# Graph attention on one core: who fetches the source rows of a group's chunks

## The chip, the core and the metric
The kernel runs on one core of a Trainium2 chip. The core has TensorE (PE), VectorE (DVE), ScalarE (ACT), GpSimd (POOL) and SyncE (SP), each with its own queue of instructions; all start DMAs onto the same 16 DMA engines. What counts is the device time of one execution in microseconds (us), as the median of several runs.

## What is computed
A graph with 6250 nodes of 128 features and 200,000 edges, sorted by destination, goes through two layers: a SAGE layer (mean over neighbours, two matrix products, a norm), then a graph attention layer with 4 heads of 32 channels. The attention layer is what matters here:

```python
x_l = (x @ W).reshape(N, H, C)
logits = leaky_relu(a_src[src_all] + a_dst[dst_all] + a_edge, 0.2)
m = segment_max(logits, dst_all)
p = exp(logits - m[dst_all])
alpha = p / segment_sum(p, dst_all)[dst_all]
out = segment_sum(alpha[:, :, None] * x_l[src_all], dst_all)
```

So for each edge the row `x_l[src]` of its source node is needed, 132 numbers (four heads of 32 channels and the head's `a_src`), 528 bytes, at a place in memory that only the data tell.

## The kernel before
The work is a row of stages; the one that the diff touches is `attention` (from line 2089), and after it comes `finish`. Edges are laid out in chunks of 128 with one edge per partition, and 15 chunks (`J`) make a group; there are 108 groups (`N_GRP`). Every engine runs the same loop over groups, unrolled 12 times (`UN`), so nine rounds; `u` is a group's place in its round. The engines meet through semaphores alone.

For a group `g`:
- **GpSimd** (line 2270) waits for `s_i` (the indices of the group are copied) and `s_ms` (its buffer is free), then issues one indirect DMA per chunk (line 2277) that gathers 128 rows of `x_tab` into a slot of `G`. `G` has room for four groups of 15 slots and two slots more. In the groups with u = 5 and 11 it leaves out the first chunk.
- **SyncE** (line 2217) issues, in each step, the load of the one-hot rows `OHT` three groups ahead (line 2222, 480 KB, in a ring of three), after a wait for `s_x`, which tells that matmuls have read the slot's last tenant. It also fetches the chunks that GpSimd leaves out: line 2255 loads that chunk's list of 128 source numbers from `src_pad` into `numbers`, line 2241 loads 16 of these at a time into registers, and line 2246 issues one DMA for each row, 16 in a part. A list is loaded at the beginning of six steps, ahead of that step's one-hots; the eight parts are spread over the six steps as 2, 2, 1, 2, 1, 0. `starts` holds where each list begins, loaded before the loop in 18 DMAs of one number (line 2229).
- **ScalarE** (line 2283) builds the one-hots of the next group from `OHT` (lines 2295, 2297), copies the indices for the group three ahead (line 2328, this signals `s_i`) and the keys `KB` (2286), then in `turned` waits for TensorE and copies `ADG` and `KT` (2302, 2306), copies edge terms (2336), and takes the exponentials `f1` (2338) and of `DL` into `PR` (2340) and `MSG` (2341). It issues no DMA in this stage.
- **TensorE** turns the logits `L` (2392), gathers destination terms (2348, and in `spread` 2363 into `px`) and sums messages by one-hot matmuls into `pu` (2375). `spread` signals `s_x`.
- **VectorE** multiplies rows with weights (`messages`, 2439, signals `s_ms`), adds up `LP` (2530, 2533), waits for the gathers of the group (`s_g`, and in groups u = 5 and 11 also `s_sr` for SyncE's rows), forms the logits `L` (2541, 2544), scans them for segment maxima (2548, 2551), builds one-hots (2433) and adds the sums of `pu` to `ACC` (2468), 15 times a group.

Before the loop, ScalarE and VectorE wait for `AE` (line 2230, 3.4 MB).

Of the kernel before, what the change touches and what calls it, by code (L numbers as in the profile page):

```python
# [149 lines left out]
def build(nc, x, src, dst, edge_attr, W1l, W1r, b1, W2l, W2r, b2, gamma, beta,  # L150
          W, W_edge, att_src, att_dst, att_edge, bias, out):
    with ExitStack() as top:
# [31 lines left out]
        rel_tab = nc.dram_tensor("rel_tab", [NK, P], BF16).ap()  # L184
        blk_tab = nc.dram_tensor("blk_tab", [1, NK], I16).ap()
        a_tab = nc.dram_tensor("a_tab", [NSL, P, N_BLK * P], BF16).ap()
        x_keep = nc.dram_tensor("x_keep", [P, NB, D], F32).ap()
# [1901 lines left out]
        def attention(at, block):  # L2089
# [7 lines left out]

            BY_SP = 6
            assert UN % BY_SP == 0 and BY_SP % 4 == 2
            s_sr = [sem(f"a_sr{u}", at) for u in range(UN // BY_SP)]  # L2100
            s_st = sem("a_st", at)
            s_nu = sem("a_nu", at)
            s_g = s_src
            s_i = sem("a_i", at)
# [44 lines left out]
            idx = sb("idx", [P, 4, J], I32, at)  # L2149
            G = sb("G", [P, 4 * J + 2, XW], F32, at)  # L2150
            starts = sb("starts", [1, N_GRP // BY_SP], I32, at)
            numbers = sb("numbers", [1, P], I32, at)
            OH = sb("OH", [P, 4, J, P], F32, at)
            OHT = sb("OHT", [P, 3, J, P], BF16, at)
# [37 lines left out]

            def by_sync(u):
                return u % BY_SP == BY_SP - 1

            def places(u):

                at_ = (0, J + 1, 2 * J + 1, 3 * J + 2)[u % 4] - (1 if by_sync(u) else 0)
                return G[:, at_:at_ + J, :]

            def fetched(i, u, last=J):

                n = [J - 1 if by_sync(v) else J for v in range(u % 4, UN, 4)]
                return 16 * (sum(n) * i + sum(n[:u // 4]) + last - (1 if by_sync(u) else 0))

# [9 lines left out]


            @block.sync
            def _(sp):
                lists = rel_tab[0:N_GRP * J].rearrange("(g j) e -> g (j e)", j=J)

                def rows_of(g, k):
                    sp.dma_start(OHT[:, k].rearrange("p j f -> p (j f)"),
                                 lists[bass.ds(g, 1), :].to_broadcast([P, J * P])).then_inc(s_rb[k], 16)

                for g in range(3):
                    rows_of(g, g)
                for r in range(N_GRP // BY_SP):
                    k = (BY_SP * r + BY_SP - 1) * J
                    sp.dma_start(starts[:, r:r + 1], ek4i[k % P:k % P + 1, k // P:k // P + 1]).then_inc(s_st, 16)
                sp.dma_start(AE[:], ae_t).then_inc(s_ael, 16)  # L2230
                sp.wait_ge(s_bz, 1)
                with nc.allow_non_contiguous_dma(reason="groups of 15 numbers"):
                    sp.dma_start(BLK[:, 2:N_GRP + 2, 0:J], blk_tab[:, 0:N_GRP * J].rearrange("o (g j) -> o g j", j=J)
                                 ).then_inc(s_bl, 16)
                sp.wait_ge(s_st, 16 * (N_GRP // BY_SP))
                flat_s = src_pad.rearrange("(o e) -> o e", o=1)
                SPAN = BY_SP - 1
                PART = 16

                def node_rows(u, at_):  # L2240
                    _, v = nc.values_load_multi_w_load_instructions(
                        numbers[0:1, at_:at_ + PART], engines=(mybir.EngineType.SP,), min_val=0, max_val=NV - 1,
                        skip_runtime_bounds_check_because="the sources are numbers of nodes")
                    for n in range(PART):
                        p = at_ + n
                        sp.dma_start(places(u)[p:p + 1, 0, :], x_tab[bass.ds(v[n], 1), :]
                                     ).then_inc(s_sr[u // BY_SP], 16)

                def round_of(i, last):
                    for half in range(UN // BY_SP):  # L2250
                        r = i * (UN // BY_SP) + half
                        u = BY_SP * half + BY_SP - 1
                        hold(sp, s_ms, BY_SP * r + 1)
                        e = sp.value_load(starts[0:1, bass.ds(r, 1)], min_val=0, max_val=(E_PAD - P) * HEADS)
                        sp.dma_start(numbers[:], flat_s[:, bass.ds(e // HEADS, P)]).then_inc(s_nu, 16)
                        for n in range(BY_SP):
                            if not last or BY_SP * half + n + 3 < UN:
                                sp.wait_ge(s_x, BY_SP * r + n + 4)
                                rows_of(BY_SP * r + n + 3, n % 3)
                            if n == 0:  # L2260
                                hold(sp, s_nu, 16 * (r + 1))
                            for at_ in range(0, P, PART):
                                if at_ // PART * SPAN // (P // PART) == n:
                                    node_rows(u, at_)

                with sp.Fori(0, N_GRP // UN - 1) as i:
                    round_of(i, False)
                round_of(N_GRP // UN - 1, True)

            @block.gpsimd  # L2270
            def _(pool):

                def step(i, u, g, left):
                    pool.wait_ge(s_i, g + 1)
                    hold(pool, s_ms, g + 1)
                    for j in range(1 if by_sync(u) else 0, END if left == 0 else J):
# [7 lines left out]
            def _(act):  # L2284
# [32 lines left out]
                turned(0)  # L2317
                act.wait_ge(s_ael, 16)

                def step(i, u, g, left):  # L2320
# [110 lines left out]
            def _(dve):  # L2431
# [5 lines left out]
                def messages(g, u, n=J):  # L2437
                    dve.wait_ge(s_p, g + 2)
                    dve.tensor_tensor(MSG[:, u % 2, 0:n, 0:XW].rearrange(x_l, h=HEADS)[:, :, :, 0:C_HEAD],  # L2439
                                      places(u % UN)[:, 0:n].rearrange(x_l, h=HEADS)[:, :, :, 0:C_HEAD],  # L2440
                                      jh(PR)[:, 0:n, :, None].to_broadcast([P, n, HEADS, C_HEAD]),
# [78 lines left out]
                def step(i, u, g, left):  # L2520
# [232 lines left out]
```

## Time and profile before

| | |
|---|---|
| median of three runs | 3497.34 us (3493.5, 3497.34, 3505.45) |
| the profiled execution, its own time | 3505.29 us |
| its span | 3503.3 us |
| VectorE busy | 2590.7 us |
| GpSimd busy | 1924.0 us |
| ScalarE busy | 1596.4 us |

The profile shows one execution. Its page gives each engine's busy time (register work, waits and issuing of DMAs do not count), the span in 40 slices, and the costliest groups of instructions by line. The list of waits says which engine waited before which line and what ended the wait. The timeline has one row per instruction or run of equal ones: start, duration, engine, line, operation, tiles, and in brackets the idle time ahead of it with its releaser. SPq and ACTq are issues of DMAs by SyncE and ScalarE, with the time of the issue, not of the transfer. A gather of GpSimd counts as DMA_INDIRECT on POOL.

### The profile page before, as it was taken

The page shows a single profiled execution, that of the slowest core. Times are in us where ns is not written, and L with a number is a line of the kernel's source. Part 1 is how long each engine was busy: PE and PEld are TensorE (multiplying, and loading weights), DVE is VectorE, ACT ScalarE, POOL GpSimd, SP SyncE. Part 2 cuts the span into 40 slices and gives each one's busy share as a digit, 9 for nine tenths or more (in the row PEclk, how much of TensorE's full clock was granted, in tenths as well). Part 3 has the DMA queues.
Part 4 walks back from the last instruction along what each step waited for, and adds up shares of the span by engine and source line. Part 5 has one row for each costly group of instructions (what it writes and reads, how often), then busy time and mean ns, then how long its engine had stood idle before and what let it go on. Part 6 is the DMA issues. An engine that isn't in the chain of part 4 may idle for free. (4 is left out here: it accounts for less than half of the span.)

```text
span 3503.3 us, 69699 instructions
## 1 busy us (share of the span) xinstructions
PE 2347.6 (67%) x19840; PEld 1970.9 (56%) x19840; DVE 2590.7 (74%) x6998; ACT 1596.4 (46%) x2523; POOL 1924.0 (55%) x1954
## 2 busy tenths in 40 slices
PE   5799999999998899455445545545555455455453
PEld 5687777888777777454444444444444444444443
DVE  4799999994576764687777767767777777777677
ACT  4587778885455556333333333333333333332331
POOL 5441111341114322477777777777777777777773
PEclk9999999999999999666665666656565665666655
DMA  5243333672378888433333333333333333333335
GB/s 171 92 168 152 140 141 151 184 172 94 120 267 250 258 256 249 155 90 79 85 84 81 82 84 84 81 82 84 84 79 84 84 79 84 85 84 78 84 78 97
DMA packets 172054, 432.24 MB, mean 123 GB/s; under 512 B 44750, under 2 KB 95768, under 8 KB 163308
## 3 DMA queue, kind: packets, MB, share of 16 engines
q1 hardware_dynamic: 62352, 271.13, 21.0%
q0 software_dynamic: 66064, 128.62, 18.9%
q10 hardware_dynamic: 43244, 27.80, 2.8%
q8 instruction: 179, 2.93, 0.4%
q14 instruction: 215, 1.76, 0.2%
HBM read 308.87 MB, written 120.11 MB: 122 GB/s over the span
## 5 line engine op out<-in xcount | busy, mean ns | idle before, releaser
L2277 POOL DMA_INDIRECT G<-x_tab,idx x1593 | 1508.5, 947 | 485.6 <-issue 485.3
L2375 PE MATMUL pu<-MSG,OH 128*128 128x140 f32 x3282 | 733.3, 395 | 26.9 <-DVEq L2505 16.4
L2375 PEld LDWEIGHTS pu<-MSG,OH 128*128 128x128 f32 x3282 | 670.7, 289 | 36.4 <-DVE ACC L2468 17.1
L2468 DVE TENSOR_TENSOR ACC<-pu,ACC 128x140 f32 x1641 | 484.1, 295 | 127.7 <-PE pu L2375 75.9
L2392 PE MATMUL pc<-ident,L 128*60 128x128 f32 x108 | 42.2, 391 | 799.1 <-DVE L L2544 789.1
L2392 PEld LDWEIGHTS pc<-ident,L 128*60 128x60 f32 x108 | 13.6, 126 | 827.1 <-issue 827.1
L961 ACT CAST AE<-psA 128x784 bf16<-128x784 f32 x496 | 397.5, 815 | 127.0 <-PE psA L994 126.0
L2302 ACT CAST ADG<-pt 128x180 bf16<-128x180 f32 x108 | 103.2, 955 | 708.4 <-PE pt L2348 702.2
L1095 DVE TENSOR_TENSOR OHL<-iol,LH 128x2048 bf16<-128x2048 bf16 (+1 forms) x248 | 358.1, 1444 | 24.2 <-PE psA L994 17.3
L1644 ACT CAST AR<-AE 128x896 fp32r<-128x896 bf16 x248 | 243.2, 1017 | 197.7 <-PE psR L1838 119.3
L1005 PE MATMUL psR<-SPL,AE 128*128 128x384 bf16 x1736 | 322.9, 326 | 0.0
L1838 PE MATMUL psR<-SPR,AR 128*128 128x256 f32 x1922 | 282.8, 295 | 10.5 <-ACT AR L1644 10.4
L994 PE MATMUL psA<-OHH_c,OHL 128*128 128x98 bf16 (+1 forms) x4800 | 259.6, 201 | 23.3 <-DVE OHH_c L1095 23.0
L1838 PEld LDWEIGHTS psR<-SPR,AR 128*128 128x128 f32 x1922 | 248.9, 193 | 23.5 <-ACT AR L1644 15.2
L2541 DVE TENSOR_TENSOR L<-G,LP 128x60 f32<-128x60 f32 x108 | 27.7, 257 | 313.3 <-DMA G<-x_tab,idx 313.3
L994 PEld LDWEIGHTS psA<-OHH_c,OHL 128*128 128x128 bf16 x4800 | 218.9, 98 | 72.0 <-DVE OHH_c L1095 35.9
L2439 DVE TENSOR_TENSOR MSG<-G,pq 128x1920 f32<-128x1920 f32 (+1 forms) x109 | 231.6, 2125 | 25.8 <-issue 25.8
L1095 DVE TENSOR_TENSOR OHH_c<-ioh,LH 128x1568 bf16<-128x1568 bf16 (+1 forms) x248 | 241.4, 973 | 0.0
L907 POOL DMA_INDIRECT srows<-src_pad,EKI x38 | 65.8, 1732 | 318.2 <-DVE KB L1077 188.5
L2433 DVE TENSOR_TENSOR OH<-pq,REL 128x1920 f32<-128x1920 f32 x108 | 232.0, 2148 | 0.0
L1830 PE MATMUL psR<-SPB,AE 128*128 128x384 bf16 x1116 | 217.6, 332 | 12.3 <-DMA AE<-a_tab 10.5
L2338 ACT ACTIVATE f<-f 1x4 f32<-1x4 f32 x108 | 22.1, 204 | 433.1 <-DVE f L2581 425.0
(432 smaller groups left out, 4453.2 us busy)
## 6 DMA issues: line engine op xcount, KB each, us to landing
a_tab<-AE SPq DMA_DIRECT2D x62, 1568.0 KB
OHT<-rel_tab SPq DMA_DIRECT2D x108, 480.0 KB, 3.9
AE<-a_tab SPq DMA_DIRECT2D x60, 800.0 KB, 6.2
AE<-a_tab SPq DMA_DIRECT2D x60, 768.0 KB, 8.6
G<-x_tab SPq DMA_DIRECT2D x2304, 0.5 KB
G<-x_tab,idx POOLq DMA_INDIRECT x1593
at_in<-in_edge_attr SPq DMA_DIRECT2D x26, 250.0 KB
SUMS<-in_edge_attr ACTq DMA_DIRECT2D x24, 250.0 KB
```

Source lines behind the costliest of these rows:

```text
L961: act.copy(A[i % 2][:, :, UN_S * u:UN_S * (u + 1)].rearrange("p h (k s) -> p k h s", k=2), psA[:, n % 2, :, 0:W8].rearrange("p k (s h) -> ...
L994: mm = pe.matmul(psA[:, n % 2, c * w // W8, to:to + w], OHL[:, m % RING, k], OHH[:, m % RING, k * step:k * step + w], start=True, stop=True)
L1005: pe.matmul(psR[:, i % 2, 0:3 * D], A[i % 2][:, h, :], SPL[:, h].rearrange("p s f -> p (s f)"), start=(h == 0), stop=False)
L1095: return dve.tensor_tensor(out.rearrange("p (s h t) -> p s h t", s=k, t=2), columns[:, 0:w].rearrange("p (h t) -> p h t", t=2)[:, None].to ...
L1644: act.copy(AR[:, n % 3, 0:len(rows_)], A[i % 2][:, rows_[0]:rows_[-1] + 1]).then_inc(s_cs, 1)
L1830: mm = pe.matmul(psR[:, i % 2, 0:3 * D], A[i % 2][:, h, :], SPB[:, h].rearrange("p s f -> p (s f)"), start=(h == 0), stop=False)
L1838: mm = pe.matmul(psR[:, i % 2, 0:2 * D], AR[:, n % 3, k], SPR[:, h - N_BF].rearrange("p s f -> p (s f)"), start=False, stop=(h == N_BLK - 1))
L2277: pool.indirect_dma_start(places(u)[:, j, :], None, x_tab, bass.IndirectOffsetOnAxis(ap=idx[:, u % 4, j:j + 1], axis=0)).then_inc(s_g[u % ...
L2375: mm = pe.matmul(pu[:, k[0], k[1]:k[1] + MW], OH[:, u % 4, j, :], MSG[:, u % 2, j, :], start=True, stop=True)
L2433: dve.tensor_tensor(OH[:, u % 4], rowq[:, None, :].to_broadcast([P, J, P]), REL[:, bass.ds(g * J, J)][:, :, None].to_broadcast([P, J, P]), ...
L2439: dve.tensor_tensor(MSG[:, u % 2, 0:n, 0:XW].rearrange(x_l, h=HEADS)[:, :, :, 0:C_HEAD], places(u % UN)[:, 0:n].rearrange(x_l, h=HEADS)[:, ...
L2468: dve.tensor_tensor(a, pu[:, k[0], k[1]:k[1] + MW][:, None, :], a, ALU.add).then_inc(s_c, 1)
```

## The change
SyncE now fetches a chunk in every fourth group (u = 3, 7, 11) instead of every sixth. A list is used in four steps with two parts in each, and it is loaded in the first of them, behind the one-hots, with the wait for it right behind its issue. The rows for u = 3 of a round are issued in the last two steps of the round before and the first two of its own, and so on, two steps ahead of their use; for the first list, two parts stand before the loop. ScalarE fetches a chunk of the group u = 9: it loads the list in step 0 of a round and issues 16 rows in each of the steps 1 to 8, between `keys` and `turned`. GpSimd gathers the others: 176 instead of 178 chunks in a round. The start of every chunk's list is now brought to one partition by a write of all 1664 numbers to a table in memory and a load of it, in place of the 18 DMAs. `G` has one slot more, and its layout changes so that the chunks fetched apart have slots that earlier groups don't use.

```diff
-            BY_SP = 6
+            BY_SP = 4
...
+            BY_ACT, PART_A = 9, 16
...
+            def chunk_apart(u):
+                if u % UN == BY_ACT:
+                    return 0
+                return None if u % 4 != 3 else 0 if u % UN == UN - 1 else J - 1
...
+            def list_of(eng, to, k, signal):
+                e = eng.value_load(starts[0:1, bass.ds(k, 1)], min_val=0, max_val=(E_PAD - P) * HEADS)
+                eng.dma_start(to[:], flat_s[:, bass.ds(e // HEADS, P)]).then_inc(signal, 16)
+
+            def node_rows(eng, kind, to, u, at_, n, signal):
+                _, v = nc.values_load_multi_w_load_instructions(
+                    to[0:1, at_:at_ + n], engines=(kind,), min_val=0, max_val=NV - 1,
+                    skip_runtime_bounds_check_because="the sources are numbers of nodes")
+                for m in range(n):
+                    eng.dma_start(places(u)[at_ + m:at_ + m + 1, chunk_apart(u), :], x_tab[bass.ds(v[m], 1), :]
+                                  ).then_inc(signal, 16)
...
+                    sp.dma_start(ek_tab.rearrange("c p -> p c"), ek4i[:]).then_inc(s_ek, 16)
                 for g in range(3):
                     rows_of(g, g)
-                for r in range(N_GRP // BY_SP):
-                    k = (BY_SP * r + BY_SP - 1) * J
-                    sp.dma_start(starts[:, r:r + 1], ek4i[k % P:k % P + 1, k // P:k // P + 1]).then_inc(s_st, 16)
+                sp.wait_ge(s_ek, 16)
+                sp.dma_start(starts[:], ek_tab.rearrange("c p -> (c p)").rearrange("(o f) -> o f", o=1)
+                             ).then_inc(s_st, 16)
                 sp.dma_start(AE[:], ae_t).then_inc(s_ael, 16)
...
+                def part(r, u, n):
+                    if n == 0:
+                        list_of(sp, numbers, (BY_SP * r + 3) * J + chunk_apart(u), s_nu)
+                        hold(sp, s_nu, 16 * (r + 1))
+                    for m in range(2):
+                        node_rows(sp, mybir.EngineType.SP, numbers, u, 32 * n + 16 * m, 16, s_sr[u // BY_SP])
 
                 def round_of(i, last):
+                    for n in range(UN):
+                        g = UN * i + n
+                        if not last or n + 3 < UN:
+                            sp.wait_ge(s_x, g + 4)
+                            rows_of(g + 3, n % 3)
+                        q = n + 2
+                        if not last or q < UN:
+                            if q % BY_SP == 0:
+                                hold(sp, s_ms, g + 2)
+                            part(UN // BY_SP * i + q // BY_SP, (q // BY_SP * BY_SP + 3) % UN, q % BY_SP)
+
+                for n in range(2):
+                    part(0, 3, n)
...
-                    for j in range(1 if by_sync(u) else 0, END if left == 0 else J):
+                    for j in gathered(u, END if left == 0 else J):
...
+                def rows_apart(i, u, g):
+                    if u == 0:
+                        list_of(act, numbers_a, g * J + BY_ACT * J, s_na)
+                    elif (u - 1) * PART_A < P:
+                        if u == 1:
+                            act.wait_ge(s_ms, g + 2)
+                            hold(act, s_na, 16 * (i + 1))
+                        node_rows(act, mybir.EngineType.Activation, numbers_a, BY_ACT, (u - 1) * PART_A, PART_A, s_ar)
...
                         keys(g + 1)
+                        rows_apart(i, u, g)
                         turned(g + 1)
...
-                    if by_sync(u):
+                    if u % BY_SP == 3:
                         dve.wait_ge(s_sr[u // BY_SP], 16 * P * (i + 1))
+                    if u == BY_ACT:
+                        dve.wait_ge(s_ar, 16 * P * (i + 1))
```

## Rows read from the trace of the kernel before

**Rows 1.** the page, busy us, share of the span and instructions of each engine
```profile
PE 2347.6 (67%) x19840; PEld 1970.9 (56%) x19840; DVE 2590.7 (74%) x6998; ACT 1596.4 (46%) x2523; POOL 1924.0 (55%) x1954
```

**Rows 2.** list of waits, 1540 to 3440 us: engine, line, releaser; us, times, longest
```profile
POOL G L2277 <- issue: 462.5, 1517, 0.3
...
DVE L L2541 <- DMA G<-x_tab,idx: 313.3, 95, 4.5
```

**Rows 3.** view of line 2277: duration ns min/median/max, first and last start us
```profile
L2277 POOL DMA_INDIRECT G<-x_tab,idx x1593: 940/944/1113, 1445.7 to 3438.6; - x200
```

**Rows 4.** timeline of VectorE, line 2541: start us, us; groups 10, 22 and 107
```profile
1670.20 0.26 DVE L2541 TENSOR_TENSOR L<-G,LP 128x60 f32<-128x60 f32 x1 [2.95 <-DMA G<-x_tab,idx]
...
1893.08 0.26 DVE L2541 TENSOR_TENSOR L<-G,LP 128x60 f32<-128x60 f32 x1 [2.96 <-DMA G<-x_tab,idx]
...
3449.11 0.26 DVE L2541 TENSOR_TENSOR L<-G,LP 128x60 f32<-128x60 f32 x1
```

**Rows 5.** timeline of SyncE, one step of its loop that waits for nobody
```profile
2593.06 0.36 SPq L2222 DMA_DIRECT2D OHT<-rel_tab  x1
2594.80 14.33 SPq L2246 DMA_DIRECT2D G<-x_tab  x32
2609.38 0.36 SPq L2222 DMA_DIRECT2D OHT<-rel_tab  x1
```

**Rows 6.** timeline of ScalarE, the two pauses in group 2498 to 2517
```profile
2509.50 0.95 ACT L2302 CAST ADG<-pt 128x180 bf16<-128x180 f32 x1 [6.61 <-PE pt L2348]
...
2514.83 0.20 ACT L2338 ACTIVATE f<-f 1x4 f32<-1x4 f32 x1 [4.08 <-DVE f L2581]
```

**Rows 7.** timeline of SyncE at the start of the stage
```profile
1445.57 10.65 SPq L2229 DMA_DIRECT2D starts<-ek4i  x18
...
1470.63 14.77 SPq L2246 DMA_DIRECT2D G<-x_tab  x32
```

**Rows 8.** timeline of SyncE around two issues of the list, within and across rounds
```profile
1553.65 0.36 SPq L2222 DMA_DIRECT2D OHT<-rel_tab  x1
1555.22 0.27 SPq L2255 DMA_DIRECT2D numbers<-src_pad  x1
...
1662.89 0.36 SPq L2222 DMA_DIRECT2D OHT<-rel_tab  x1
1668.26 0.27 SPq L2255 DMA_DIRECT2D numbers<-src_pad  x1
```

**Rows 9.** the page, DMA issues: KB each, median us from issue to landing
```profile
OHT<-rel_tab SPq DMA_DIRECT2D x108, 480.0 KB, 3.9
```

**Rows 10.** timeline of SyncE, the last 64 rows
```profile
3390.90 30.62 SPq L2246 DMA_DIRECT2D G<-x_tab  x64
```

**Rows 11.** timeline of VectorE, line 2541, groups 0 and 5
```profile
1483.07 0.26 DVE L2541 TENSOR_TENSOR L<-G,LP 128x60 f32<-128x60 f32 x1
...
1558.66 0.26 DVE L2541 TENSOR_TENSOR L<-G,LP 128x60 f32<-128x60 f32 x1 [0.93 <-DMA G<-x_tab,idx]
```

**Rows 12.** list of DMA issues of ScalarE, two kinds that are small
```profile
x_tab<-H ACTq DMA_DIRECT2D x1, 66.0 KB, 1.6
...
b1c<-in_L_gnn_b ACTq DMA_DIRECT2D x1, 1.0 KB, 12.2
```

**Rows 13.** views of lines 2241 and 2246: SyncE loading 16 numbers, issuing a row
```profile
L2241 SPq TENSOR_LOAD <-numbers x144: 1137/1180/1407, 1469.3 to 3413.4; - x144
...
L2246 SPq DMA_DIRECT2D G<-x_tab x2304: 224/228/293, 1470.6 to 3421.3; - x192
```

**Rows 14.** view of line 2452: VectorE loading eight block numbers
```profile
L2452 DVEq TENSOR_LOAD <-BLK x219: 1823/1828/2056, 1470.4 to 3451.9; - x110
```

**Rows 15.** views of lines 2722, 2654 and 2658: both engines issuing after the stage
```profile
L2722 SPq DMA_DIRECT2D X<-x_keep x3: 363/425/427, 3468.1 to 3468.9; - x3
...
L2654 ACTq DMA_DIRECT2D H<-x_tab x4: 407/528/532, 3467.8 to 3469.3; - x4
...
L2658 ACTq DMA_DIRECT2D H<-x_tab x9: 374/851/1611, 3470.6 to 3477.6; - x9
```

More of the change, by code:

```diff
@@ L185, in build @@
         blk_tab = nc.dram_tensor("blk_tab", [1, NK], I16).ap()
+        ek_tab = nc.dram_tensor("ek_tab", [KC, P], I32).ap()
         a_tab = nc.dram_tensor("a_tab", [NSL, P, N_BLK * P], BF16).ap()
@@ L2095, in attention @@
             assert N_GRP % UN == 0
-            BY_SP = 6
-            assert UN % BY_SP == 0 and BY_SP % 4 == 2
+            BY_SP = 4
             s_sr = [sem(f"a_sr{u}", at) for u in range(UN // BY_SP)]
+            s_ek = sem("a_ek", at)
             s_st = sem("a_st", at)
             s_nu = sem("a_nu", at)
+            BY_ACT, PART_A = 9, 16
+            s_ar = sem("a_ar", at)
+            s_na = sem("a_na", at)
             s_g = s_src
@@ L2149, in attention @@
             idx = sb("idx", [P, 4, J], I32, at)
-            G = sb("G", [P, 4 * J + 2, XW], F32, at)
-            starts = sb("starts", [1, N_GRP // BY_SP], I32, at)
+            G = sb("G", [P, 4 * J + 3, XW], F32, at)
+            starts = sb("starts", [1, NK], I32, at)
             numbers = sb("numbers", [1, P], I32, at)
+            numbers_a = sb("numbers_a", [1, P], I32, at)
             OH = sb("OH", [P, 4, J, P], F32, at)
@@ L2191, in jh, with gathered @@
                 return t.rearrange("p h j -> p j h")
-            def by_sync(u):
-                return u % BY_SP == BY_SP - 1
+            def chunk_apart(u):
+                if u % UN == BY_ACT:
+                    return 0
+                return None if u % 4 != 3 else 0 if u % UN == UN - 1 else J - 1
             def places(u):
-                at_ = (0, J + 1, 2 * J + 1, 3 * J + 2)[u % 4] - (1 if by_sync(u) else 0)
+                if u % 4 == 3:
+                    at_ = 3 * J + {UN - 1: 1, 3: 2, 7: 3}[u % UN]
+                else:
+                    at_ = (0, J + 1, 2 * J + 1)[u % 4] - (1 if u % UN == BY_ACT else 0)
                 return G[:, at_:at_ + J, :]
+            def gathered(u, last=J):
+                return [j for j in range(last) if j != chunk_apart(u)]
             def fetched(i, u, last=J):
-                n = [J - 1 if by_sync(v) else J for v in range(u % 4, UN, 4)]
-                return 16 * (sum(n) * i + sum(n[:u // 4]) + last - (1 if by_sync(u) else 0))
+                n = [len(gathered(v)) for v in range(u % 4, UN, 4)]
+                return 16 * (sum(n) * i + sum(n[:u // 4]) + len(gathered(u, last)))
             def steps(eng, body):
@@ L2213, in steps @@
                     body(rounds, u, UN * rounds + u, UN - 1 - u)
+            flat_s = src_pad.rearrange("(o e) -> o e", o=1)
+            def list_of(eng, to, k, signal):
[8 more added lines that the diff above has]
+                                  ).then_inc(signal, 16)
             @block.sync
@@ L2223, in rows_of @@
                                  lists[bass.ds(g, 1), :].to_broadcast([P, J * P])).then_inc(s_rb[k], 16)
+                with nc.allow_non_contiguous_dma(reason="chunks lie along partitions"):
+                    sp.dma_start(ek_tab.rearrange("c p -> p c"), ek4i[:]).then_inc(s_ek, 16)
                 for g in range(3):
                     rows_of(g, g)
-                for r in range(N_GRP // BY_SP):
-                    k = (BY_SP * r + BY_SP - 1) * J
-                    sp.dma_start(starts[:, r:r + 1], ek4i[k % P:k % P + 1, k // P:k // P + 1]).then_inc(s_st, 16)
+                sp.wait_ge(s_ek, 16)
+                sp.dma_start(starts[:], ek_tab.rearrange("c p -> (c p)").rearrange("(o f) -> o f", o=1)
+                             ).then_inc(s_st, 16)
                 sp.dma_start(AE[:], ae_t).then_inc(s_ael, 16)
@@ L2234, in _ @@
                                  ).then_inc(s_bl, 16)
[L2235 to L2247, printed above, removed]
@@ L2249, in round_of @@
-                def round_of(i, last):
[L2250 to L2264, printed above, removed]
+                hold(sp, s_st, 16)
@@ L2318, in _ @@
                 act.wait_ge(s_ael, 16)
+                act.wait_ge(s_st, 16)
+                def rows_apart(i, u, g):
[6 more added lines that the diff above has]
+                        node_rows(act, mybir.EngineType.Activation, numbers_a, BY_ACT, (u - 1) * PART_A, PART_A, s_ar)
                 def step(i, u, g, left):
@@ L2439, in messages @@
                     dve.tensor_tensor(MSG[:, u % 2, 0:n, 0:XW].rearrange(x_l, h=HEADS)[:, :, :, 0:C_HEAD],
-                                      places(u % UN)[:, 0:n].rearrange(x_l, h=HEADS)[:, :, :, 0:C_HEAD],
+                                      places(u)[:, 0:n].rearrange(x_l, h=HEADS)[:, :, :, 0:C_HEAD],
                                       jh(PR)[:, 0:n, :, None].to_broadcast([P, n, HEADS, C_HEAD]),
```

## The prediction

> **What bounds the kernel now.** The page's busy shares come first [rows 1]: no engine is busy for more than 74% of the span, so averages don't name the bound. The stage that the diff touches is `attention`, 108 groups of up to 15 chunks in about 2000 us of the 3503. The list of waits in the stage does [rows 2]: VectorE waits for a landing of `G` before line 2541 in 95 groups, 313.3 us in all, so some 3.3 us a group, while GpSimd's only waits are "issue", 0.3 us before each gather. The view of line 2277 says the same from the other side [rows 3]: 1593 gathers from 1445.7 to 3438.6 us, so one in 1.252 us (944 ns and the gap). GpSimd issues without a pause and is the clock of the stage. Line 2541 confirms it [rows 4]: between 1670.20 and 1893.08 us, twelve groups or one round of the loop, lie 222.88 us, and the 178 gathers of a round at 1.252 us make 222.9.
>
> Two other clocks run close behind, and the change loads both. SyncE issues the rows that GpSimd doesn't gather. Where it waits for nobody, a step with 32 rows takes 2609.38 - 2593.06 = 16.3 us [rows 5], against 222.88 / 12 = 18.6 us for a group. ScalarE has two pauses in a group, 6.6 us before `ADG` and 4.1 us before `f` [rows 6].
>
> **What is taken from GpSimd.** Before, two groups in twelve (u = 5, 11) lack a gather: 178 in a round. After, u = 3, 7, 11 and 9 lack one: 176. In nine rounds that is 18 gathers fewer, 1575 in all, and 18 x 1.252 = 22.5 us. The rest of GpSimd's step is unchanged: its waits on `s_i` and `s_ms` were met ahead. All 22.5 us lie on the path as long as the next clock is slower by no more than that, so the stage's last full wait, and with it the last `L`, moves from 3449.1 us [rows 4] to 3426.6.
>
> **SyncE, the main question.** A step of its loop issues the rows of one-hots (line 2222), then up to 32 rows. Before, a list served six steps, with 2, 2, 1, 2, 1 and 0 parts of 16 rows. The full steps were followed by lighter ones. Now a list serves four steps, each with two parts. Four steps cost:
> - Four full steps. 16.3 each where all runs freely [rows 5]; but the 32 rows themselves take 14.33 to 14.77 us [rows 5, 7], so I take 16.6 and have 66.5, with 65.3 as the lower bound.
> - The list. Without a turn of the loop, `numbers` is issued 1.57 us after the rows of one-hots, of which 0.36 is their own issue: 1.2 us [rows 8]. Before, it was issued ahead of the next one-hots and a whole step's wait hid its landing. Now it is issued behind them, on the same queue, and `hold` on `s_nu` follows at once. One-hots take 3.9 us from issue to landing [rows 9]; a list behind them lands no earlier, so at least 3.9 - 1.6 = 2.3 us are waited. If it takes a whole such landing of its own it is 3.9. With the 1.2 that is 3.5 to 5.1; I take 4.0, nearer the first, as the list is one row of 0.5 KB against 480.
> - The turn of the loop. 1668.26 - 1662.89 = 5.37 us where it is otherwise 1.57 [rows 8]: 3.8 us in twelve steps, 1.3 in four.
> Together 71.8 us, bounds 70.1 and 72.9.
>
> GpSimd's four groups will cost (222.88 - 2.5) / 3 = 73.5 us. So SyncE fits, by 2%. It also starts late: its first list waits behind the load of `AE`, and rows start at 1470.63 [rows 7]. Now 64 rows come before the loop, where one-hots of group 3 were issued at once; 64 rows take 30.6 us [rows 10]. So the loop's first step begins near 1501.3. One-hots of group 3 go out there, 16 us or so ahead of ScalarE's use; the rows of groups 3 and 7 come some 5 to 10 us after GpSimd's, which VectorE makes good, since its own work is (1558.66 - 0.93 - 1483.07) / 5 = 14.9 us a group while it waits for nobody [rows 11]. Rows of the last group are out after 106 steps, 26.5 fours: 1501.3 + 26.5 x 71.8 + 1.6 for landing (the fastest landing of a plain DMA [rows 12]) = 3405.6, against 3426.6. The break-even is (3426.6 - 1.6 - 1501.3) / 26.5 = 72.6 us in four steps. Below it SyncE costs nothing; every us above costs 26.5 us at the end.
>
> **ScalarE.** In eight of twelve steps it issues 16 rows between `keys` and `turned`. By SyncE's rows that is 1.2 us of load [rows 13] and 16 x 0.41 (14.33 us for 32 with a load between) = 7.8 us. The pause there is 6.6 us and the next, before `f`, 4.1 [rows 6]; `ADG` itself is read only by matmuls after that. So 7.8 against 10.7 us: `ADG` is late by 1 us and nobody sees it. The bounds: its load of 16 numbers may cost twice VectorE's load of 8 at 1.83 us [rows 14], which makes 10.2, still inside; nothing is gained on this side. `list_of` in step 0 is some 1.5 us in the same pause. What is queued behind it is `turned`, then the copy of `AE`, `f`, and the weights for VectorE's messages.
>
> **The start.** SyncE's 18 issues of 4 bytes, 10.65 us [rows 7], go. In their place stand a write of 1664 single numbers to `ek_tab`, a wait for it, and one load of all starts, ahead of `AE`. No row shows such a write; its bounds are 1.6 us, that fastest landing, and 12.2, a load of 256 single numbers [rows 12], so `AE` starts between some 8 us earlier and 3 later. VectorE does group 0 at 1483.07, 17 us after its gathers could be in, and waits for one again only in group 5 [rows 11]; nor is SyncE's margin of 21 us used up. So this is worth nothing; GpSimd starts as before. One more slot of `G` and a longer `starts` cost no time.
>
> **Sum.** The profiled execution has 3505.3 us for a span of 3503.3; with 22.5 less it would be 3482.8. That execution lies 8.0 above the median of the three runs, which scatter over 12. Against the median: 3497.3 - 22.5 = 3475.
>
> **Rivals.**
> A. *SyncE and ScalarE get in each other's way, and SyncE becomes the bound.* The end of the trace has both issuing at once [rows 15]: SyncE's three issues go from 363 to 427 ns, ScalarE's four from 407 to 532, while ScalarE alone has one of the same shape in 374. If an issue of SyncE's costs 62 ns more whenever ScalarE issues, that is 7.8 of 18.4 us in two steps of three, or 28% of 128 rows, 36 x 0.062 = 2.2 us in four steps; with ScalarE itself slowed to 10 us, 2.9. Then 71.8 + 2.2 = 74.0, the end moves by 26.5 x 1.4 = 37 us, and the time is 3475 + 37 = 3512: slower than before. It decides from 72.6 for a loss of gain, and from 73.45 for a loss against the kernel before. Against it: those issues are of 128 rows each, these of one row with 228 ns [rows 13], in which whatever is shared can be only a small part; with a third of that surcharge SyncE stays within 0.1 us of break-even. The same end is reached if the list lands later than 5 us after its issue.
> The Trainium skill, Perfetto Trace Analysis, section "DMA Instruction — HWDGE (DVE, Sync)", speaks for this rival: the generator of descriptors is shared and is locked for one issuer at a time, and the wait for the lock is within the time the profile gives for the issue. The longer issues at the end of the trace agree with it. If all 228 ns of a row were spent under that lock, two engines would get one row each per 456 ns, 0.045 more than SyncE's 0.41, and by the same sum the time would be 3475 + 26.5 x (71.8 + 1.6 - 72.6) = 3496.
> B. *SyncE is the bound without ScalarE's doing*, by late lists and stalls: at the upper bound of 72.9 it costs 8 us, 3483, still faster.
> C. *ScalarE is the bound.* If its rows begin only after `KB`, its load costs 3.7 us and each row 0.15 more, it issues for 12.6 us. That is 1.9 beyond the 10.7 of pauses, in 72 groups: 137 us, 3612. It decides from 10.7 us. Nothing in the trace shows ScalarE's issues slower than SyncE's by more than 20% when alone.
> D. *Nothing is gained*: gathers become dearer, or landings later, with more rows in flight. Against it: 940, 944 and 1113 ns are least, middle and most of 1593 gathers [rows 3], though SyncE's rows were in flight beside most of them. 3497.
>
> **Chances.** GpSimd stays the bound: 0.52, and 3475. SyncE the bound by little (B, and A in a mild form), up to 3487: 0.10. A between 3487 and 3508, and D: 0.16. A above 3508: 0.17. C: 0.05. For 3475 alone the range would be 3466 to 3484 by the scatter of runs; for 8 in 10 it must take in most of A, so 3466 to 3522. A measurement tells about 0.3% (10.5 us) from no change: faster 0.62, same 0.16, slower 0.22.
>
> **What would show it.** 1575 gathers at 944 ns, and line 2541 at 220.4 us per round, still waiting for GpSimd's `G`, by some 2 us more in groups of 15 than in those of 14. SyncE's step of 16.6 us, a list step of about 20.6, and SyncE still waiting now and then for `px`, though far less than before. Were A right, SyncE would hardly wait, line 2541 would wait in groups u = 3, 7, 11 for SyncE's rows, GpSimd would pause before the first gather of groups, and issues at the new line of rows would be well over 228 ns. Were C right, the pause before `f` would be gone and VectorE would wait for `px` or `PR`.

## The result and the profile after

The changed kernel takes 3483.1 us (median of six runs, 3477.7 to 3486.2); the kernel before, measured beside it, 3504.2. The ratio is 0.9938 with a 95% interval of 0.9919 to 0.9958: 21 us or 0.6% faster. The forecast was 22.5 us less, 3475 us, with a range of 3466 to 3522. The median is 8 us above the forecast because the kernel before also measured 7 us more over six runs than over the three that were known; the gain itself is 1.4 us short of the forecast.

The profiled execution has a span of 3475.5 us, 27.8 less than before. Of that, 4.8 us are not the change's: its first gather lies at 1440.85 us instead of 1445.69, though no stage ahead was edited, and in the runs below it lies anywhere from 1435.3 to 1449.9 (but for one whose edit moves it). What belongs to the change is the way from the first gather to the last `L`: 3449.1 - 1445.7 = 2003.4 us before, 3421.1 - 1440.9 = 1980.2 after, so 23.2 us less. That stretch, called "the stage" below, is the measure in all runs, since a single execution gives it to about 2 us: four executions of programs that come to the same have 1980.2 to 1982.1 (see the extra loads below). The 1980.2 of the changed kernel is the lowest of them, so its gain in the stage is 21.3 to 23.2 us.

The views of GpSimd's gathers (line 2305, was 2277 [rows 3]) and of VectorE's line for `L` (2583, was 2541), with duration in ns and first and last start:

```profile
L2305 POOL DMA_INDIRECT G<-x_tab,idx x1575: 940/944/1106, 1440.9 to 3410.6; - x197
...
L2583 DVE TENSOR_TENSOR L<-G,LP x108: 246/258/296, 1480.1 to 3421.1; 128x60 f32<-128x60 f32 x108
```

1575 gathers where there were 1593, and one in (3410.6 - 1440.9) / 1574 = 1.251 us as before. The list of waits, 1540 to 3420 us, whose counterpart is [rows 2]:

```profile
ACT ADG L2330 <- PE pt L2388: 546.4, 84, 12.6
POOL G L2305 <- issue: 455.7, 1494, 0.3
ACT f L2378 <- DVE f L2623: 367.8, 101, 4.4
DVE L L2583 <- DMA G<-x_tab,idx: 246.1, 80, 5.2
...
ACT ADG L2330 <- issue: 116.0, 19, 7.4
```

GpSimd still pauses for nothing but its own issuing. VectorE waits for its gathers 246 us instead of 313. ScalarE's two pauses had been, in the same list of the kernel before, 1540 to 3440 us:

```profile
ACT ADG L2302 <- PE pt L2348: 680.4, 102, 8.2
...
ACT f L2338 <- DVE f L2581: 400.5, 100, 4.4
```

After, 546.4 + 116.0 us are ahead of `ADG` and 367.8 ahead of `f`, but the list counts the issuing of the 1152 rows as pause. What tells of room is the releaser: in 84 groups `ADG` waits for TensorE as before, in 19 for ScalarE's own issuing. A new row of VectorE's list, over the whole stage, stands for SyncE's lateness in the first rounds:

```profile
DVE L L2583 <- DMA G<-x_tab: 45.7, 6, 9.3
```

Six groups wait for SyncE's rows (3, 7, 11, 15, 19 and 23), the last of them at 1883.67 us; none later does. Together VectorE waits 246.1 + 45.7 = 291.8 us for `G`, 21.5 less than before. What SyncE waits for, 1440 to 3420 us:

```profile
SPq L95 <- DMA numbers<-src_pad: 51.8, 27, 9.9
...
SPq L2255 <- PE px L2403: 33.4, 21, 2.4
```

All 33.4 us for TensorE's `px` lie behind 2000 us: until then SyncE, once its rows have begun, pauses for nothing but its lists. SyncE itself, in the timeline while it is behind (issue of the one-hots, of the list, of 32 rows):

```profile
1585.55 0.36 SPq L2255 DMA_DIRECT2D OHT<-rel_tab  x1
1587.28 14.62 SPq L2247 DMA_DIRECT2D G<-x_tab  x32
1602.15 0.36 SPq L2255 DMA_DIRECT2D OHT<-rel_tab  x1
1603.68 0.27 SPq L2239 DMA_DIRECT2D numbers<-src_pad  x1
1606.90 14.79 SPq L2247 DMA_DIRECT2D G<-x_tab  x32
1621.94 0.36 SPq L2255 DMA_DIRECT2D OHT<-rel_tab  x1
...
1745.85 0.27 SPq L2239 DMA_DIRECT2D numbers<-src_pad  x1
```

A full step is 16.6 us (1585.55 to 1602.15), the step with the list 19.8 (1602.15 to 1621.94). The list before this one is issued at 1534.78; three fours later comes that at 1745.85, so four steps cost 211.1 / 3 = 70.4 us, turns of the loop included. (A step with a turn takes 19.6 us instead of 16.6, so a turn costs 3.0.)

### The profile page after: what moved, and what is told of

It is laid out like the page before. It is cut to its first block and busy times, and to the rows that moved or that the text cites. A ratio compares the mean times of both kernels' runs of the same rounds, so it can differ in the third digit from the quotient of the medians.

```text
span 3475.5 us, 76894 instructions
## 1 busy us (share of the span) xinstructions
PE 2347.6 (68%) x19840; PEld 1970.5 (57%) x19840; DVE 2587.4 (74%) x6998; ACT 1596.8 (46%) x2524; POOL 1907.6 (55%) x1936
## 5 line engine op out<-in xcount | busy, mean ns | idle before, releaser
L2305 POOL DMA_INDIRECT G<-x_tab,idx x1575 | 1490.6, 946 | 480.2 <-issue 479.6
L2415 PE MATMUL pu<-MSG,OH 128*128 128x140 f32 x3282 | 734.8, 396 | 17.7 <-DVE ACC L2508 11.6
L2583 DVE TENSOR_TENSOR L<-G,LP 128x60 f32<-128x60 f32 x108 | 27.8, 257 | 291.8 <-DMA G<-x_tab,idx 246.1
L2323 ACT ACTIVATE OHT<-OHT,mine 128x1920 bf16<-128x1920 bf16 x108 | 204.1, 1890 | 12.0 <-DMA OHT<-rel_tab 12.0
```

Source lines behind the costliest of these rows:

```text
L2305: pool.indirect_dma_start(places(u)[:, j, :], None, x_tab, bass.IndirectOffsetOnAxis(ap=idx[:, u % 4, j:j + 1], axis=0)).then_inc(s_g[u % ...
L2415: mm = pe.matmul(pu[:, k[0], k[1]:k[1] + MW], OH[:, u % 4, j, :], MSG[:, u % 2, j, :], start=True, stop=True)
```

## The experiments

In each, only what is named differs from the changed kernel.

### One part alone, the other undone

Without ScalarE's part:

```diff
-                if u % UN == BY_ACT:
-                    return 0
...
-                        rows_apart(i, u, g)
...
-                    if u == BY_ACT:
-                        dve.wait_ge(s_ar, 16 * P * (i + 1))
```

> The changed kernel without ScalarE's part: GpSimd gathers the chunk of u = 9 again, 177 in a round, 1584 in all. Theory (GpSimd is the clock, every gather costs 1.252 us): from the first gather to the last L (VectorE's line after the wait for G) 1980.2 + 9 x 1.252 = 1991.5 us, a time 11 us above the changed kernel. Rival (the engines' issues get in each other's way): SyncE's step with 32 rows becomes clearly shorter than the 14.6 us of rows it has in the changed kernel, towards 14.3 or less, and its lists come closer together than 70.4 us while it is behind; the loss of ScalarE's chunk would then be partly made good, under 8 us. By the theory SyncE's pitch between rows stays at 0.411 us.

Measured: a ratio to the kernel before of 0.9985 (0.9967 to 1.0003), and a stage of 3441.2 - 1445.9 = 1995.3 us, 4 above the theory: 15 us more than the changed kernel where 11.3 were expected. Its gathers:

```profile
L2303 POOL DMA_INDIRECT G<-x_tab,idx x1584: 941/947/1123, 1445.9 to 3430.8; - x198
```

They are 947 ns long at the median instead of 944 and come one in 1.2539 us instead of 1.2514; on 1584 gathers that is 4.0 us, the whole difference. SyncE's lists, while it is behind, are issued at 1539.39 and 1608.39 us, 69.0 apart, where the changed kernel has 1603.68 - 1534.78 = 68.9; over the first three whole rounds it is 211.4, 211.3 and 211.5 us against 211.1, 211.5 and 211.1. The trace of the changed kernel shows the same row by row: of SyncE's 3456 issues 858 overlap in time with an issue of ScalarE's, and these take 229.0 ns on average, the other 2598 take 229.4. So 16 rows a step by ScalarE do not slow SyncE measurably. Rival A falls.

Without SyncE's rows:

```diff
-                return None if u % 4 != 3 else 0 if u % UN == UN - 1 else J - 1
+                return None
...
-                            part(UN // BY_SP * i + q // BY_SP, (q // BY_SP * BY_SP + 3) % UN, q % BY_SP)
...
-                    if u % BY_SP == 3:
-                        dve.wait_ge(s_sr[u // BY_SP], 16 * P * (i + 1))
```

> The changed kernel in which SyncE fetches no rows; ScalarE's chunk stays. GpSimd gathers 179 in a round, 1602 in all. Theory (GpSimd is the clock): 27 x 1.252 = 33.8 us more than the changed kernel, so 2014.0 us from the first gather to the last L, and some 11 us more than the kernel before. Rival (SyncE's rows in flight make gathers or landings dearer): the gathers come faster than one in 1.252 us and the stage is clearly shorter than 2014, say under 2008. VectorE's waits for SyncE's rows in the first rounds go.

Measured: ratio 1.0015 (0.9998 to 1.0032); the stage is 3450.6 - 1435.3 = 2015.3 us against 2014.0. Again its gathers are 947 ns long:

```profile
L2301 POOL DMA_INDIRECT G<-x_tab,idx x1602: 940/947/1089, 1435.3 to 3441.4; - x178
```

With 3456 rows fewer in flight the gathers are no cheaper, so rival D falls too: within 3 ns, the price of a gather does not hang on who else has rows under way. From this kernel to the one without ScalarE's part are 18 gathers and 20.0 us (18 pitches are 22.6, but its pitch is 1.2530 us against 1.2539, and its last `L` follows the last gather after 9.2 us instead of 10.4), from there to the changed kernel 9 gathers and 15.1, of which 4.0 are the 3 ns.

### The list issued ahead of the one-hots

```diff
+                def list_for(r, u):
+                    list_of(sp, numbers, (BY_SP * r + 3) * J + chunk_apart(u), s_nu)
...
+                        if (not last or q < UN) and q % BY_SP == 0:
+                            hold(sp, s_ms, g + 2)
+                            list_for(UN // BY_SP * i + q // BY_SP, (q // BY_SP * BY_SP + 3) % UN)
                         if not last or n + 3 < UN:
                             sp.wait_ge(s_x, g + 4)
                             rows_of(g + 3, n % 3)
```

> As the changed kernel, but SyncE issues its list ahead of the one-hots of that step, so that it lands while SyncE waits for TensorE or issues the one-hots. Theory (SyncE isn't the bound): SyncE's list step gets shorter by 2 to 3 us, so four steps cost 68 us where they cost 70.4 while it is behind, it catches up rounds earlier, and the stage is unchanged, 1980 us within 1.5. Rival (SyncE's lateness in the first rounds costs something at the end): the stage gets shorter by 5 us or more.

The stage is 3420.9 - 1439.7 = 1981.2 us: unchanged. Issues of one-hots around a list:

```profile
1533.24 0.36 SPq L2255 DMA_DIRECT2D OHT<-rel_tab  x1
1535.25 14.68 SPq L2247 DMA_DIRECT2D G<-x_tab  x32
1550.17 0.36 SPq L2255 DMA_DIRECT2D OHT<-rel_tab  x1
```

The step that uses a list now takes 1550.17 - 1533.24 = 16.9 us from one issue of one-hots to the next, instead of 19.5 to 19.8, but the issue of the list has only moved to the step before, which takes 18.2 us instead of 16.6. Three lists further it is 207.4 us instead of 211.1, so four steps cost 69.1 us, 1.2 less and not the 2.4 that were expected. Four groups instead of six wait for SyncE's rows. Its lateness was paid out of VectorE's slack and nothing else, as far as 1.2 us in four steps can tell.

### Extra loads that were not there

Three kernels were to slow SyncE by loads of 16 numbers that nobody reads.

```diff
+                    for _ in range([1, 1, 1, 1][n]):
+                        nc.values_load_multi_w_load_instructions(
+                            numbers[0:1, 0:16], engines=(mybir.EngineType.SP,), min_val=0, max_val=NV - 1,
...
```

> The changed kernel; SyncE loads 16 numbers once more in one step of four, 1.25 us with nothing gained, so four of its steps cost 70.4 + 1.25 = 71.7 us. In the changed kernel the first of its loop's steps begins at 1499.85 us, and GpSimd's clock puts the last L at 3421.1, so the break-even is (3421.1 - 1.6 - 1499.85) / 26.5 = 72.4 us. Theory (below the break-even SyncE costs nothing): 1980 us from the first gather to the last L, within 4, with SyncE's waits for TensorE nearly gone. Rival (SyncE is already part of the clock): its 26.5 x 1.25 = 33 us show in part, 1990 us or more.

> As before, but two extra loads in four steps: 72.9 us, 0.5 beyond the break-even of 72.4. Theory: 26.5 x 0.5 = 13 us more than the changed kernel, 1993 us from the first gather to the last L. Rival (SyncE had more room than reckoned): 1980.

> One extra load in every step of SyncE: 75.4 us in four, 3.0 beyond the break-even. Theory (every us beyond it costs 26.5): 80 us more, 2060 us from the first gather to the last L, a time slower than the kernel before; VectorE waits in the groups u = 3, 7 and 11 for SyncE's rows up to the end, and its waits for GpSimd's gathers go. Rival (the two clocks give way to each other, a late list costs only its own group): clearly less, under 2030.

The stages were 1981.3, 1982.1 and 1981.5 us. That tells nothing of the theory, for the loads are not in the trace; the kernel with four of them has as many as the changed one, 216:

```profile
L2243 SPq TENSOR_LOAD <-numbers x216: 1131/1222/1421, 1476.4 to 3396.2; - x108
```

The loads into registers that nothing uses are not part of the program that runs here. What the three are good for is the scatter: with the changed kernel they make four equal programs in effect, with stages from 1980.2 to 1982.1 us.

### SyncE slowed, this time with DMAs

```diff
+                    if [1, 1, 1, 1][n]:
+                        hold(sp, s_sp, 16 * (4 * r + {0: 0, 1: 1, 2: 2, 3: 3}[n] + 1))
+                        list_of(sp, spare, (BY_SP * r + 3) * J + chunk_apart(u), s_sp)
```

> The changed kernel; in two steps of four SyncE loads a list into a spare buffer that nobody reads, 1.4 us each by the changed kernel's trace (0.45 for the number, 0.27 for the issue, the rest between), so four steps cost 70.3 + 2.8 = 73.1 us. With one gather less per group the last L came at 3352.9 us, on SyncE's last row; GpSimd's clock puts it at 3421.1. The break-even is so 70.3 + 68.2 / 26.5 = 72.9 us. Theory: 0.2 beyond, 5 us more than the changed kernel, 1981 to 1990 us from the first gather to the last L. Rival (every us of SyncE's counts): 26.5 x 2.8 = 74 us more, 2054.

> As before, with the spare list in every step: 70.3 + 5.6 = 75.9 us in four steps, 3.0 beyond the break-even of 72.9. Theory: 26.5 x 3.0 = 80 us more than the changed kernel, 2060 us from the first gather to the last L, slower than the kernel before; VectorE waits for SyncE's rows in the groups u = 3, 7 and 11 up to the end. Rival (the clocks give way to each other): under 2030.

The views of SyncE's rows and of VectorE's `L`, first with two spare lists in four steps, then with four:

```profile
L2249 SPq DMA_DIRECT2D G<-x_tab x3456: 224/228/282, 1470.1 to 3437.5; - x192
...
L2590 DVE TENSOR_TENSOR L<-G,LP x108: 242/252/292, 1480.9 to 3438.7; 128x60 f32<-128x60 f32 x108
```

```profile
L2249 SPq DMA_DIRECT2D G<-x_tab x3456: 224/228/414, 1471.5 to 3517.9; - x192
...
L2590 DVE TENSOR_TENSOR L<-G,LP x108: 240/251/263, 1481.3 to 3519.1; 128x60 f32<-128x60 f32 x108
```

In both the last `L` starts 1.2 us after SyncE's last row, and VectorE waits for SyncE's rows in all 27 groups that have them, 313.9 and 394.9 us in all, and for GpSimd's in none: the path runs on SyncE. GpSimd's last gather in the first of them lies at 3412.1 us, at its old pace. The stages are 3438.7 - 1441.8 = 1996.9 and 3519.1 - 1442.6 = 2076.5 us, 17 and 96 more than in the changed kernel, where 5 and 80 were expected.

What four steps cost: in the changed kernel SyncE's loop starts 1499.85 - 1469.2 = 30.65 us after its first row, in these two 32.0. So over the 26.5 fours up to the last row it is (3437.5 - 1470.1 - 32.0) / 26.5 = 73.0 and (3517.9 - 1471.5 - 32.0) / 26.5 = 76.0 us. (From a list to the third one after it, in the middle of the run, it is 220.4 / 3 = 73.5 and 229.3 / 3 = 76.4; the average over the whole is 0.4 lower, mostly because the last fours, without a turn of the loop, are shorter.)

In the changed kernel 28.3 us lie between the first gather and SyncE's first row, then the 30.65, and a last row is followed by `L` after 1.2: 60.2 us. So SyncE sets the end when 26.5 fours take more than 1980.2 - 60.2 us, beyond 72.4 to 72.5 us each. That agrees with the sum made before the first of these runs, and lies 0.2 below the prediction's 72.6. The expectations had 72.9, from a kernel in which SyncE starts 6 us earlier (the next section), which was not allowed for.

That each us beyond it costs 26.5 us is the number of fours and so follows once SyncE is the bound; what the runs add is that it is, without any give: 2076.5 - 1996.9 = 79.6 us for two spare lists more in four steps, which the middle of the run prices at 8.9 / 3 = 2.97 us, 26.8 to one. The second kernel took 3575.5 us in its one execution, well above the kernel before.

### One gather less in every group

```diff
-                return [j for j in range(last) if j != chunk_apart(u)]
+                return [j for j in range(last) if j != chunk_apart(u) and j != 2]
```

The rows of that chunk are not fetched, so its messages are left out of the sums. `G` is cleared ahead of the loop, and SyncE and GpSimd wait for that.

> The changed kernel; GpSimd leaves one more chunk of each group out altogether (its rows are not fetched; the slots are cleared once at the start), 108 gathers less. GpSimd alone would gain 108 x 1.252 = 135 us, to 1845 us from the first gather to the last L. Theory (SyncE is the next bound, at 70.4 us in four groups): the last L comes at SyncE's time, 59 + 26.5 x 70.4 + 1.6 = 1926 us after the first gather, a gain of 54 us, and GpSimd idles about 80 us. Rival (no second bound so near): 1845 us, or VectorE's 15 us a group as the bound, even less than that.

The views of GpSimd's gathers, SyncE's rows and VectorE's `L` with the waits ahead of it:

```profile
L2307 POOL DMA_INDIRECT G<-x_tab,idx x1467: 940/945/1126, 1460.7 to 3304.4; - x184
...
L2248 SPq DMA_DIRECT2D G<-x_tab x3456: 224/228/333, 1463.5 to 3351.7; - x192
...
L2586 DVE TENSOR_TENSOR L<-G,LP x108: 245/254/261, 1480.5 to 3352.9; 128x60 f32<-128x60 f32 x108
...
  DMA G<-x_tab: 199.1, 24
  DMA G<-x_tab,idx: 28.5, 15
```

The clearing moved the first gather by some 20 us, so here the ends are compared: `L` starts in group 0 at 1480.5 (1480.1 in the changed kernel) and in the last group at 3352.9 against 3421.1, 68 us earlier and not 135. VectorE waits for rows fetched apart 24 times, nearly all of them SyncE's (7 to 8 us on average in the groups u = 3, 7 and 11, 0.1 in u = 9), and no longer much for GpSimd. SyncE is the next bound, at (3351.7 - 1463.5 - 30.65) / 26.5 = 70.1 us for four groups. It came 14 us earlier than expected, since its rows began 6 us earlier and its four steps cost 0.3 less than 70.4 over the whole; in the middle of the run they cost 70.4 as before.

### ScalarE slowed

```diff
+                        hold(act, s_sp, 80 * (8 * i + u - 1) + 16)
+                        for m in range(5):
+                            list_of(act, spare[:, m], g * J, s_sp)
                         node_rows(act, mybir.EngineType.Activation, numbers_a, BY_ACT, (u - 1) * PART_A, PART_A, s_ar)
```

> The changed kernel; ScalarE loads five spare lists ahead of its 16 rows in each of its eight steps, 7.5 us. It then issues for 7.3 + 7.6 = 14.9 us, from 1.7 us before the end of its copy of the keys, against a pause of 6.6 before ADG, 4.0 before f and the 1.7. Theory (ScalarE becomes the bound of these steps): ADG and then f are late by 2.6 us, VectorE's wait for GpSimd is used up, a step with rows costs 20.8 us where GpSimd needs 18.3, and the four light steps, at 15 us, don't make it good: 8 x 20.8 + 4 x 14.9 = 226 us in a round against 219.9, some 55 us more, 2035 from the first gather to the last L. Rival (nobody sees it, as in the changed kernel): 1980.

The list of waits, 1540 to 3440 us:

```profile
ACT ADG L2332 <- issue: 924.2, 70, 13.6
...
PE px L2410 <- issue: 431.2, 70, 6.7
...
DVE f L2639 <- ACT f L2384: 298.6, 64, 5.1
```

The stage is 3471.0 - 1447.4 = 2023.6 us, 43 more than in the changed kernel, 55 expected. VectorE waits for no landing any more but for ScalarE's `f`, 4.7 us in each of 64 groups. So ScalarE's room is real and ends about where the sum of the two pauses says: 12 us of the 55 did not come. Rival C is a cliff that the change keeps clear of.

### Two chunks a round by ScalarE

If GpSimd is the clock and ScalarE has room, ScalarE can take a second chunk.

```diff
-            BY_ACT, PART_A = 9, 16
+            BY_ACT, PART_A = (4, 10), 22
...
+                    n = (u + 2) % 6
+                    k = 0 if u < 4 or u >= 10 else 1
+                    if left is None or u < 10:
+                        if n == 0:
+                            act.wait_ge(s_ms, g - 1)
+                            hold(act, s_na, 16 * (2 * (i + (1 if u >= 10 else 0)) + k + 1))
+                        rows_part(k, n)
+                    if n == 5 and (left is None or u < 9):
+                        list_of(act, numbers_a[:, 1 - k], g * J + 7 * J + J - 1, s_na)
```

> ScalarE fetches two chunks a round, those of u = 4 and u = 10, in all twelve steps, 22 rows in each (18 in every sixth), its first 44 rows ahead of the loop, its lists in two buffers; GpSimd gathers 175 in a round, 1566 in all. SyncE as in the changed kernel. Theory (GpSimd is the clock and ScalarE has room): ScalarE issues for 1.5 + 22 x 0.373 = 9.7 us from 1.7 us before the end of its copy of the keys, so it is done about when ADG can start. The stage is 9 x 1.252 = 11.3 us shorter than in the changed kernel, 1969.0 us, and the time some 11 us below it. Rival (ScalarE becomes the bound): ADG and f late, the pause before f gone, and a time equal to the changed kernel's or above.

Ratio to the kernel before 0.9910 (0.9887 to 0.9932), median 3476.5 us. The stage is 3421.6 - 1448.5 = 1973.1 us, 7.1 less than in the changed kernel, not 11.3. GpSimd's timeline names 2.8 of the missing 4 us:

```profile
1507.58 0.94 POOL L2305 DMA_INDIRECT G<-x_tab,idx  x1 [3.14 <-ACT idx L2379]
```

It is the first gather of group 3: its indices are copied in ScalarE's step 0, which began late behind the 44 rows issued before the loop. So these were moved ahead of the wait for `AE`:

```diff
+                act.wait_ge(s_st, 16)
+                list_of(act, numbers_a[:, 0], 4 * J + J - 1, s_na)
+                hold(act, s_na, 16)
+                for n in range(2):
+                    rows_part(0, n)
                 act.wait_ge(s_ael, 16)
```

> ScalarE fetches two chunks a round as in the kernel with u = 4 and u = 10, and its first 44 rows are issued before its wait for AE, not behind it. There, GpSimd paused 2.8 us before its 46th gather, as the indices of group 3 came late from ScalarE. Theory: the first rows lie beside the load of AE, the pause goes, and the stage is 1566 gathers at 1.252 us long, 1969 to 1971 us from the first gather to the last L; the time 2 to 3 us below that kernel's and some 30 us below the kernel before. Rival (the pause has another cause): 1973 as there.

The pause is gone and the stage is shorter by 2.7 us:

```profile
L2305 POOL DMA_INDIRECT G<-x_tab,idx x1566: 940/944/1126, 1446.2 to 3406.0; - x196
...
L2595 DVE TENSOR_TENSOR L<-G,LP x108: 245/257/278, 1485.2 to 3416.6; 128x60 f32<-128x60 f32 x108
```

That is 3416.6 - 1446.2 = 1970.4 us. The ratio to the kernel before is 0.9906 (0.9892 to 0.9920), the median 3473.2 us: 0.9% faster than the kernel before, and 9.8 us shorter in the stage than the changed kernel. From the first version with two chunks the medians don't tell it apart (0.9910). Its list of waits shows what it has used up:

```profile
ACT ADG L2330 <- issue: 1040.4, 103, 11.9
...
POOL G L2305 <- issue: 453.9, 1488, 0.3
DVE L L2595 <- DMA G<-x_tab,idx: 185.2, 70, 5.6
```

VectorE still waits 185 us for gathers; ahead of `ADG` ScalarE waits for its own issuing in 103 groups and hardly for TensorE any more. In both versions with two chunks SyncE gets a little slower: from a list to the third one after it, over the first three rounds, it takes 211.4 to 212.4 us in the first and 212.4 to 213.5 in the second, against 211.1 to 211.5 in the changed kernel. The rows are not dearer (229 ns each); it is the steps with a list that are longer.

## Why the prediction was right

- **GpSimd is the clock, and each gather costs 1.252 us.** Right. Counts of 1566, 1575, 1584 and 1602 gathers gave stages of 1970.4, 1980.2, 1995.3 and 2015.3 us, with 3 ns more per gather at the median in the last two.
- **22.5 us, all on the path.** 23.2 in the profiled execution, 21 in the medians, and 21.3 to 23.2 over the four executions that come to the same.
- **SyncE fits by 2%.** Right in kind, and the terms can be told apart. Full steps were taken as 16.6 us and measured 16.3 to 16.7. The list was the term that was mis-sized: 4.0 us were taken, with 3.5 as the lower bound, and about 3.0 are there (19.5 to 19.8 less 16.6). SyncE waits for its 27 lists 51.8 us in all, 9.9 of them for the first, so 1.6 us each for the others, where at least 2.3 were reckoned. That a list can't land before the one-hots ahead of it on the queue was the wrong step, as far as it can be told: the list is there some 3.4 us after the issue of the one-hots (1602.15 to 1605.6, where the wait for it ends), whose own landing took 3.9 in the kernel before and is not in this kernel's trace. The turn of the loop was taken as 1.3 us in four steps and is 1.0. Four steps came to 70.4 in the middle of the run, and to 70.1 as the average of 26.5, instead of 71.8. The break-even was put at 72.6 and is 72.4, also as such an average. So the margin was 2.3 us in four steps, not 0.8, and SyncE's 70.4 against GpSimd's 73.4 (176 x 1.2514 / 3) is 4%, not 2.
- **SyncE's late start is made good by VectorE.** Right: waits in six groups up to 1884 us, none after, and no change in the end when SyncE is made 1.2 us faster in four steps.
- **ScalarE is hidden.** Right, with the size on the safe side: 1.2 us of load and 6.1 for 16 rows, 7.3 instead of 7.8, and the first row goes out while the arithmetic ahead of it still runs. But the room is used in part, as forecast: in 27 of the 72 steps with rows `ADG` follows the last row within 0.3 us, and starts up to 3.2 us after `pt` is ready; the pause before `f` is never under 0.9 us in these steps, and VectorE doesn't see it. In the other 45 the last row is out ahead of `ADG`, by 1.5 us at the median. A group with more than most:

```profile
2375.47 0.46 ACTq L2247 DMA_DIRECT2D G<-x_tab  x1
2375.71 0.19 ACT L2367 CAST idx<-SRC 128x15 int32 x1
2375.80 0.24 ACT L2314 COPY KB<-KEY 128x60 f32 x1
2376.09 5.44 ACTq L2247 DMA_DIRECT2D G<-x_tab  x15
2384.48 0.96 ACT L2330 CAST ADG<-pt 128x180 bf16<-128x180 f32 x1 [8.44 <-PE pt L2388]
```

- **The start is worth nothing.** Right. `AE` is issued 11.6 us after SyncE's first issue; it was 12.0 before. Group 0's `L` comes 39.3 us after the first gather, instead of 37.4, which VectorE makes good with the rest.
- **Rival A, the shared generator.** It was read from large DMAs at the end of the trace [rows 15] and carried over to single rows. The reading was weak in itself: after SyncE's last issue there, ScalarE alone issues nine more, of which only the first takes 374 ns and the others 634 to 1611, so long issues of such DMAs need no second issuer. With and without ScalarE's rows SyncE's lists are 68.9 and 69.0 us apart, its issue is 228 ns at the median in both, and where issues of the two overlap they are no longer than elsewhere (229.0 and 229.4 ns). The Trainium skill's rule of a locked generator (Perfetto Trace Analysis, "DMA Instruction — HWDGE (DVE, Sync)") may hold, but no run here shows a cost of it for DMAs of one row. The measurement rules out that all 228 ns of a row are spent under such a lock, which the prediction priced at 3496. Most of the chance of a slower kernel rested on this rival, and that was too much; a SyncE that is too slow has the price that was told, but from 2.3 us more in four steps on.

What stays open: why the gathers of two programs took 947 ns instead of 944, which is 4.0 us of stage in one and 2.6 in the other (a pitch of 1.2539 and 1.2530 us against 1.2514); they ran on the same chip as two with 944, and differ from these in which engines issue rows, but also in the code around, and that was not tried apart. The other 1.4 us of the 4 that were missing in the first version with two chunks remain in the second, too; they are within the 2 us by which programs that come to the same differ.

## What to carry to other kernels

When one engine issues without a pause, work taken from it is worth its pitch times the count, and the question is what the takers have left: give each taker a clock of its own (us per period, waits, lists and turns of the loop included) and a break-even against the first clock. Below the break-even a taker costs nothing even if it is late for a while (here in its first six groups); beyond it every microsecond counts in every period. An engine with pauses between its computations can issue DMAs in them, and it can start earlier than the timeline of its computations suggests.

## What was not expected of the hardware

- ScalarE issues single-row DMAs faster than SyncE: 217 ns and one in 0.373 us ((5.44 - 0.22) / 14), against 228 ns and 0.411 at the median on SyncE.
- The first such DMA of each step, behind ScalarE's activations, takes 0.45 to 0.54 us in all 72 steps, the following ones 0.22.
- Two engines issuing single rows at once do not slow each other's issues: SyncE's 858 that overlap with one of ScalarE's take 229.0 ns on average, its others 229.4.
- A write of 1664 single numbers to memory, issued in 0.39 us, held SyncE for 9.2 us until it had landed, and the one-hots issued right behind it reached ScalarE 14.5 us after their issue, where it had been 4.0 before.
